# Transposing the rotated q and k ahead of the probabilities, and copying them out in that order

## The reference

```
x = x + layernorm(mixer(layernorm(x)))      # gated linear recurrence over the tokens
x = x + layernorm(ffn(layernorm(x)))
# ffn: two layers of
h = shift_token(x);  q, k, v = split(h @ wqkv)           # 8 heads of 64
q, k = rotary(l2norm(q) * qs), rotary(l2norm(k) * ks)
o = local_attention(q, k, v)      # windows of 64 queries, 128 keys, masked softmax
x = x + o @ wo
h = layernorm(shift_token(x)) * lg + lb
a, g = split(h @ w1 + b1);  x = x + (a * gelu(g)) @ w2 + b2
```

## Time and profile before

| | |
|---|---|
| median of 3 runs | 407.89 us (407.08 to 412.19) |
| profiled execution, its own time | 410.05 us |
| its span, first to last instruction | 408.2 us |
| busy share of the span | PE 85%, DVE 80%, POOL 70%, ACT 69% |
| mean granted TensorE clock | 0.946 of full |

### The profile page before, as it was taken

One profiled execution on the slowest core, in us unless ns is written; L12 is line 12 of the kernel. 1 busy time (PEld: TensorE's weight loads), 2 busy tenths in 40 slices (PEclk: granted clock), 3 DMA queues, 4 the chain that ended last, 5 costly groups with the idle time before them and its releaser, 6 DMA issues.

```text
span 408.2 us, 10765 instructions
## 1 busy us (share of the span) xinstructions
PE 349.0 (85%) x3856; PEld 290.9 (71%) x3856; DVE 325.8 (80%) x766; ACT 283.1 (69%) x864; POOL 285.7 (70%) x223
## 2 busy tenths in 40 slices
PE   1558358789999999999999999999999999987781
PEld 0346247677888788878888888888888888866561
DVE  4687966998889688968896889688969897945653
ACT  1846247789998778877887787778787868755320
POOL 5532777998987978788875887588858986870222
PEclk9988758899999999999999999999999999998966
DMA  7801101522422043205320532053204310220110
GB/s 231 280 4 40 39 2 27 144 59 59 119 65 58 10 125 84 66 3 142 70 64 2 149 68 58 3 149 79 48 2 124 86 39 1 60 62 0 27 51 26
DMA packets 40682, 27.84 MB, mean 68 GB/s; under 512 B 20483, under 2 KB 34870, under 8 KB 40630
## 3 DMA queue, kind: packets, MB, share of 16 engines
q1 hardware_dynamic: 40630, 27.16, 26.1%
HBM read 13.51 MB, written 2.89 MB: 40 GB/s over the span
## 4 chain that ended last, share of the span: by engine, by line
PE 54%; DVE 24%; ACT 11%; issue 6%; POOL 1%; DMA 1%; SPq 0%; POOLq 0%; DVEq 0%; ACTq 0%
PE bank L717 7%; PE upper L674 5%; PE upper L700 5%; PE bank L759 5%; PE upper L680 5%; PE bank L560 4%; ACT probs L924 3%; PE bank L564 3%; PE upper L650 3%; PE bank L561 3%; DVE ss L1181 3%; PE bank L641 3%; PE upper L641 3%; DVE o_tok L1235 2%; DVE rot_sin L1168 2%
## 5 line engine op out<-in xcount | busy, mean ns | idle before, releaser
L924 ACT ACTIVATE probs<-upper,neg_max 128x128 f32<-128x128 f32 x256 | 90.6, 370 | 40.6 <-DVE neg_max L1223 40.6
L516 POOL TENSOR_TENSOR rot<-rot_cos,rot_sin 128x512 f32<-128x512 f32 x64 | 82.1, 1305 | 41.0 <-DVE rot_sin L1168 31.3
L481 POOL TENSOR_TENSOR rn<-floored,minus_half 128x16 f32<-128x16 f32 x32 | 93.8, 2932 | 23.1 <-DVE floored L1184 23.1
L527 POOL TENSOR_TENSOR rot<-rot,rn 128x1024 f32<-128x1024 f32 x32 | 61.0, 1906 | 2.5
L1223 DVE TENSOR_REDUCE neg_max<-upper 128x4 f32<-128x512 f32 x64 | 43.1, 684 | 12.6 <-PE upper L700 12.5
L924 ACT ACTIVATION_READ_ACCUMULATOR probs<-upper,neg_max 128x1 f32 x256 | 53.1, 208 | 0.0
L560 PE MATMUL bank<-wqkv_hi,act_t_hi 128*128 128x512 f32 x96 | 43.5, 453 | 9.2 <-DVE o_tok L1235 3.6
L1168 DVE TENSOR_TENSOR rot_cos<-bank,tab 128x512 f32<-128x512 f32 x64 | 43.7, 682 | 1.7 <-DVE y L1261 1.3
L973 ACT ACTIVATE sq<-bank 128x512 f32<-128x512 f32 x64 | 36.8, 614 | 11.4 <-DVE rot_sin L1168 11.4
L1168 DVE TENSOR_TENSOR rot_sin<-bank,tab 128x512 f32<-128x512 f32 x64 | 43.6, 680 | 0.0
L674 PE MATMUL upper<-const,probs 128*128 128x128 f32 x256 | 35.4, 280 | 6.2 <-ACT probs L924 5.0
(11 more groups left out here) (159 smaller groups left out, 834.5 us busy)
## 6 DMA issues: line engine op xcount, KB each, us to landing
v_mid<-v_tok SPq DMA_DIRECT2D x64, 128.0 KB, 2.4
tab_raw<-tables SPq DMA_DIRECT2D x8, 512.0 KB, 3.6
h_tok<-group_in SPq DMA_DIRECT2D x14, 128.0 KB, 3.3
x_res<-group_in SPq DMA_DIRECT2D x28, 64.0 KB, 1.8
wqkv_raw<-wqkv SPq DMA_DIRECT2D x2, 768.0 KB, 8.3
x_in<-x SPq DMA_DIRECT2D x4, 256.0 KB, 4.4
head_scale<-head_scales SPq DMA_DIRECT2D x8, 128.0 KB, 3.9
group_in<-y SPq DMA_DIRECT2D x4, 256.0 KB
```

Of the source, the lines that this page charges most:

```text
L481: pool.tensor_tensor(rn[:, 0:2 * HEADS], floored[:, 0:2 * HEADS], minus_half[:, :], ALU.pow).then_inc(rn_ready, 1)
L516: pool.tensor_tensor(halves(rot[cur.par]), halves(rot_cos), halves(rot_sin)[:, :, ::-1, :], ALU.add).then_inc(rot_added, 1)
L527: pool.tensor_tensor(rot[cur.par][:, :, :], rot[cur.par][:, :, :], rn[:, 0:2 * HEADS].unsqueeze(2).broadcast_to([P, 2 * HEADS, DH]), ALU.m ...
L924: last = act.activation(probs[:, h, :], s_bank[half][:, (h % 4) * P:(h % 4 + 1) * P], ACT.Exp, bias=neg_max[a.par][:, h:h + 1], accum_out= ...
```

## The change

In PE's step `transpose_qk(prev)` moves ahead of the two `transpose_probs(mid, ...)`, together with the wait for `y_read` that j = 3 has. In ACT's step `save_probs(mid)` moves behind the copies of q and k (and behind `carry_keys`). Nothing is added or removed, and DVE, POOL and SP keep their order. The end of the program, after the last full step, is as it was.

```diff
@@ PE, body
                     if after.valid:
                         project_out(after)
-                    if mid.valid:
-                        transpose_probs(mid, 0)
-                        transpose_probs(mid, 1)
                     if prev.valid:
                         if j == 3:
                             pe.wait_ge(y_read, G + 1)
                         transpose_qk(prev)
+                    if mid.valid:
+                        transpose_probs(mid, 0)
+                        transpose_probs(mid, 1)
                     if done.valid:
                         transpose_o(done)
@@ ACT, body
                     if cur.t == 0:
                         late_weights()
-                    if mid.valid:
-                        save_probs(mid)
                     if prev.valid:
                         act.wait_ge(qt_done, prev.t + 1)
                         need(act, s_done, 2 * prev.t)
@@
                         if prev.slot == GT - 1 and prev.group < LAST - 1:
                             carry_keys(prev)
+                    if mid.valid:
+                        save_probs(mid)
                     if done.valid:
                         save_o(done)
```

## The result

The changed kernel takes 437.14 us (median of 4 runs, 436.34 to 439.09); the kernel before, its three runs and one taken beside these, 410.04 us (407.08 to 412.30). The ratio is 1.067, with a 95% interval of 1.061 to 1.073: slower. The profiled execution took 436.71 us, in a span of 434.9 us; forecast were 437.0 in 435.1.

A forecast was written before the change was run, and what follows sets the result against it. The prediction took PE as the bound, busy 39.66 of 40.30 us per four-step group. Its terms, 12.5 + 7.6 + 2.6 + 3.8 + 0.4 = 26.9 us, on 407.89 us gave 434.8 us, range 426 to 441.

The forecast's parts named there:

- PE counts, and ACT's copy ends last: In the steady groups PE's waits are paid in full; ACT's probabilities copy has no slack, 195.17 against 195.23.
- 0.96 us in j = 0 and j = 2: ACT's q and k copies, 0.48 us each, delay the probabilities copy in 13 steps, adding 12.5 us.
- Hidden wait for POOL: PE waits 0.5 us for POOL's multiplication before transposing q and k, hidden behind ACT with 0.3 us to spare.
- 1.27 us in j = 1: ACT's q and k copies plus 0.31 us of carried keys delay the values in six steps, adding 7.6 us.
- 0.44 us in j = 3: After the feed-forward ACT is early, so only 0.44 us is paid in each of six steps, 2.6 us.
- First steps, 3.8 us: At t = 2 to 6 DVE's later copies and ACT's queue add 3.8 us, with bounds 1.8 and 4.6.
- Last step, 0.4 us: At t = 32 POOL's multiplication keeps the transposes from filling PE's wait; 0.4 us, with bounds 0 and 0.96.
- The median, 434.8 us: Predicted median of the changed kernel's runs: 407.89 us before plus 26.9 us.
- Rival A: Transposes of q and k fill PE's wait for ACT's exponentials; not slower, 403 us if all is regained; chance 4%.
- Rival D: Idle time elsewhere on PE, 0.64 us in each of seven groups, absorbs part: 425 us; chance 4%.
- Rival C: PE's clock falls to 1.2 GHz after the new waits, once in each of seven groups: 445 us; chance 5%.
- Rival B: A closed path through PE's transposes, DVE and POOL, 9.0 to 9.1 us, becomes the bound: 440.5 us; chance 10%.

The follow-up runs named there:

- The run with one copy: The kernel before, with only ACT's copy of q moved ahead of its copy of the probabilities: 421.91 us, ratio 1.030.
- the sums first: The changed kernel with DVE's sums of squares put ahead of its copy of the probabilities: 440.83 us, ratio 1.077.
- the first experiment: The changed kernel's PE order with ACT's order of the kernel before, probabilities copied first: 435.21 us, ratio 1.062.

## Why the prediction was right

- **PE counts, and ACT's copy ends last.** Right. The 22 short waits of the earlier trace rows marked the place, and it is where 30.6 us of waiting came.
- **0.96 us in j = 0 and j = 2.** Right: 0.97 to 0.99, but for two steps with j = 0 (t = 27 and 31) at 1.2. The run with one copy shows the price as 0.48 us for each copy, the run with ACT's order alone shows the two. Why t = 27 and 31 cost 0.2 us more was not tried. In the step ahead of them DVE also computes the output's variances, and its next maxima begin 1.58 us behind the masks (330.29 to 331.87), where in the group before it is 1.35 (286.27 to 287.62): 0.23 us, which fits.
- **Hidden wait for POOL.** Right: forecast were a wait of 0.5 us and 0.3 us to spare behind it, measured 0.41 and 0.35. That it is hidden was argued from times ahead of the run. Two runs show it from either side: taken away it brings nothing (the sums first), and ACT's order without it costs as much as the whole. That it is no small thing for being hidden, PE's order alone shows, with 26 us.
- **1.27 us in j = 1.** Right: 1.25, and the carried keys are 0.27 of it, by the run in which they stand behind.
- **0.44 us in j = 3.** Slightly low: 0.45 to 0.55, six times. With it the forecast's own terms make a group of 43.9 us (40.3 + 0.96 + 1.27 + 0.96 + 0.44), not the 43.8 that it names; measured are 44.1.
- **First steps, 3.8 us.** Too high: 2.46, or 2.97 from t = 2 on. At t = 5 nothing is added (-0.08), since ACT's rows of the lead-in took in the shift, where I had expected DVE's division to pass it on: the masks of t = 4 are 1.57 us later than before, ACT's first exponential of t = 5 only 0.48 (93.38 and 93.86), and the two copies make up the rest. At t = 3 the kernel before ran its products of q, k and v and the transposes at the lower clock (below), and its value products began 0.5 us behind the end of ACT's copy (78.54 and 79.04). So up to 0.5 us of the low figure is no merit of the order.
- **Last step, 0.4 us.** Right in size and in cause: L641 waits 2.71 us for POOL and 0.45 us are added. POOL's path is 9.14 us there (379.77 to 388.91). The size is in part luck: with the same wait and the lower clock behind it, the run with the carried keys behind added 1.94 us in this step.
- **The median, 434.8 us.** Too low by 2.3. I took the profiled execution to lie 2.2 us above the median, as in the kernel before; the changed kernel's lies 0.4 us below its own. Against the median of the runs beside them (410.04 us) the change costs 27.1 us, where 26.9 was forecast.
- **Rival A** (transposes fill the wait for the exponentials) is out as a whole. At t = 5, 6 and 32 they did fill it, 3.0 of 5.0 us, but PE then waited for ACT's copy instead, at t = 32 for POOL. **Rival D** (slack on PE) is out: j = 3 paid in full. **Rival C** (clock) did not come in the steady groups, which stayed at 1.00; it did at t = 32 in four of the experiments. **Rival B** is the one that was nearest: had ACT's order been left alone, it would have been the whole cost, at 3.0 us a group. My price for it on its own, in the first experiment, was 8 us too low or more. The path itself I had nearly right, 9.0 to 9.1 us where it is 9.08 to 9.19 and once 9.43. What I missed were DVE's wait in j = 2 (0.4 us a group), the first steps (3.5 us) and the last one (3.7 us, of which about 2.6 is the clock).

The sum came out at 26.9 against 26.6 us with errors that nearly cancel: 1.3 us too much in the first steps and 1.0 us too little in the steady ones. That it agrees to 0.3 us is luck; the terms of the steady steps, 22.7 us against 23.7, are what was understood.

## What to carry to other kernels

A wait of 0.2 us that recurs in two thirds of the steps is a sign that two engines arrive together. Here whatever was put ahead of the releasing instruction on its queue was paid at its full time, per copy, except in j = 3 of the changed kernel, where ACT had been about 0.5 us early. Two such costs that lie side by side ahead of one wait did not add, so undoing half of a bad change may bring back almost nothing, as each half here costs 26 and 28 us alone, and both together 27. And a price argued from the time of one closed path has to be checked in the steps at both ends, where the work that usually covers it is missing.

## What the runs showed that was not expected

The granted clock after a wait of PE is not fixed by the length of the wait. At t = 3 the kernel before ran the products of q, k and v at the lower level after 2.41 us; the changed one waited longer there and ran at the higher:

```profile
74.93 0.47 PE L560 MATMUL bank<-wqkv_hi,act_t_hi 128*128 128x512 f32 x1 [2.87 <-DVE o_tok L1235]
```

At t = 32 above, 2.71 us were followed by four transposes in 0.66 us, and 2.70 us by four in 1.11. The forecast's evidence against rival C was one wait of 1.26 us without a fall. The kernel before has the same two waits, 1.26 and 0.78 us, once more, 8 us later, and there the clock fell behind the second:

```profile
369.33 0.66 PE L674 MATMUL upper<-const,probs 128*128 128x128 f32 x4 [1.26 <-ACT probs L924]
370.76 0.83 PE L674 MATMUL upper<-const,probs 128*128 128x128 f32 x4 [0.78 <-ACT probs L924]
371.38 1.06 PE L650 MATMUL upper<-const,o_tok 128*128 128x128 f32 x4
```

What decides it is not shown. From L641 to the masks of t = 32 it was 3.4 us at the higher level, 4.9 with the fall in the run with the carried keys behind, and 6.0 in the one with PE's order alone, so programs that hardly differ there can lie 1.5 to 2.6 us apart. A total that is to be read to 1 us needs the steady period from the trace, not the end time.
